# Self-attention of a two-layer block: the products of probabilities and values are put between the next transposes of probabilities, with both parts of the probabilities in one wide product

## What is computed

```python
def _layer(x, wqkv, qs, ksc, wo, ...):
    h = shift_token(x)                  # second half of the features comes from the token before
    q, k, v = split(h @ wqkv, 3)        # 8 heads of 64
    q = l2norm(q) * qs
    k = l2norm(k) * ksc
    q, k = rotary_xpos(q, k)
    o = local_attention(q, k, v)        # a query sees the 256 keys before it and its own
    x = x + o @ wo
    ...                                 # layer norm, w1, gelu gate, w2
```

## Time and profile before

| | |
|---|---|
| time, median of 3 runs | 3539.25 us (3538.21 to 3539.43) |
| time of the profiled execution | 3536.69 us |
| its span | 3534.9 us |
| PE busy | 3405.1 us, 96% |
| PEld busy | 2790.6 us, 79% |
| DVE busy | 1950.2 us, 55% |
| ACT busy | 1701.9 us, 48% |
| POOL busy | 1135.6 us, 32% |
| mean granted TensorE clock | 0.991 of full speed |

### The profile page before, as it was taken

How to read it: one execution, slowest core, us unless ns; L and a number is a source line. 1 busy time by engine, 2 the same in 40 slices (tenths; PEclk the granted TensorE clock), 3 DMA queues, 4 the chain that set the end, 5 groups by cost and what they waited for, 6 DMA issues and landing times. The chain is left out here.

```text
span 3534.9 us, 56378 instructions
## 1 busy us (share of the span) xinstructions
PE 3405.1 (96%) x20560; PEld 2790.6 (79%) x20560; DVE 1950.2 (55%) x4487; ACT 1701.9 (48%) x4490; POOL 1135.6 (32%) x1011
## 2 busy tenths in 40 slices
PE   6999998999999999999999979999999899999999
PEld 5666676788888877888888868888888778888887
DVE  6888876777777764222332257776777543323232
ACT  5666664777677762111111147776777521111111
POOL 3433434555555520000000045555555121110011
PEclk9999999999999999999999999999999999999999
DMA  4112204111111132011111111111111421101111
GB/s 124 42 46 65 72 34 135 49 61 61 61 61 61 61 97 93 29 41 44 44 43 44 65 66 61 61 61 61 61 61 58 129 93 50 49 34 50 50 34 37
DMA packets 186917, 216.26 MB, mean 61 GB/s; under 512 B 27142, under 2 KB 125702, under 8 KB 186643
## 3 DMA queue, kind: packets, MB, share of 16 engines
q1 hardware_dynamic: 186643, 212.65, 18.8%
HBM read 125.79 MB, written 69.00 MB: 55 GB/s over the span
## 5 line engine op out<-in xcount | busy, mean ns | idle before, releaser
L1981 DVE SCALAR_TENSOR_TENSOR u_full<-banks,b_cols,gate 128x512 f32<-128x512 f32 (+1 forms) x176 | 132.1, 751 | 876.7 <-ACT gate L1939 802.5
L1939 ACT ACTIVATE gate<-banks,b_cols 128x512 f32<-128x512 f32 (+1 forms) x176 | 121.3, 689 | 1010.8 <-PE banks L48 1010.8
L46 PE MATMUL banks<-fxT_h,w_h 128*128 128x512 f32 (+1 forms) x1408 | 556.7, 395 | 3.1 <-DVE w_l L1965 2.4
L48 PE MATMUL banks<-fxT_h,w_l 128*128 128x512 f32 (+1 forms) x1408 | 556.8, 395 | 0.0
L47 PE MATMUL banks<-fxT_l,w_h 128*128 128x512 f32 (+1 forms) x1408 | 556.0, 395 | 0.0
L1834 POOL TENSOR_TENSOR sums<-sums,b_rows 128x512 f32<-128x512 f32 x64 | 85.5, 1368 | 877.8 <-DMA sums<-z_rows 877.8
L46 PE MATMUL banks<-wqkv_h,hT_h 128*128 128x512 f32 x768 | 323.8, 422 | 9.7 <-DVE hT_l L1497 7.6
L46 PEld LDWEIGHTS banks<-fxT_h,w_h 128*128 128x128 f32 (+1 forms) x1408 | 260.2, 185 | 70.8 <-DVE w_l L1965 3.7
L48 PEld LDWEIGHTS banks<-fxT_h,w_l 128*128 128x128 f32 (+1 forms) x1408 | 260.8, 185 | 67.4
L47 PEld LDWEIGHTS banks<-fxT_l,w_h 128*128 128x128 f32 (+1 forms) x1408 | 260.4, 185 | 67.1
L48 PE MATMUL banks<-wqkv_h,hT_l 128*128 128x512 f32 x768 | 303.7, 395 | 0.0
(11 more groups left out here) (192 smaller groups left out, 8084.0 us busy)
## 6 DMA issues: line engine op xcount, KB each, us to landing
y_rows<-sums SPq DMA_DIRECT2D x16, 1024.0 KB
sums<-y_rows SPq DMA_DIRECT2D x64, 256.0 KB, 2.9
z_rows<-sums SPq DMA_DIRECT2D x64, 256.0 KB, 2.0
sums<-z_rows SPq DMA_DIRECT2D x16, 1024.0 KB, 5.6
thirds<-in_w SPq DMA_DIRECT2D x30, 512.0 KB, 5.0
thirds<-in_x SPq DMA_DIRECT2D x8, 1024.0 KB, 6.9
thirds<-y_rows SPq DMA_DIRECT2D x64, 128.0 KB, 2.7
thirds<-y_late SPq DMA_DIRECT2D x64, 128.0 KB, 3.3
```

What stands on the lines that cost most here:

```text
L46: pe.matmul(out, a_h, b_h, start=start, stop=False)
L48: return pe.matmul(out, a_l, b_h, start=False, stop=stop)
L1939: e.activation(gate[r, :], ps[r, 2 * (m % 2) + 1, :], ACT.Gelu, bias=b1[r, place[m], 1:2]).then_inc(s["ac_g"], 1)
L1981: e.scalar_tensor_tensor(out=u_full[r, m % 2, :], in0=ps[r, 2 * (m % 2), :], scalar=b1[r, place[m], 0:1], in1=gate[r, :], op0=ALU.add, op1 ...
```

## The change

Only the order and the shape of work in self-attention change, and one semaphore in the feed-forward part.

- `pT` becomes one tensor that holds high part and rest side by side (`[P, 4, 2, KEYS]`). For each key block, `weigh` makes one matmul of the high part of v by 256 columns, which are both parts of the probabilities; `weigh_rest` makes one of v's rest by 128 columns (the high part). The two results lie side by side in PSUM and take two banks instead of one, so `lo_o` now takes four VectorE instructions a half instead of two: it subtracts the high part into `o_rest`, and then adds the second result.
- `turn_and_weigh(t, half)` takes the place of four `transpose_p` and four `values`. Between the transposes of tile t, half 1 it puts the values of half 0 of the same tile; between those of half 0 the values of half 1 of the tile before.
- TensorE's list in tile t becomes: turn_and_weigh(t, 0), transpose_qk(t+1) for k, project(t+2, 0), scores(t+1, 0), project(t+2, 1), turn_and_weigh(t, 1), output(t-1), scores(t+1, 1), transpose_qk(t+2) for q, project(t+2, 2), transpose_h(t+3). At the end a `turn_and_weigh(NT, 0)` with values alone stands between two halves of output(30).
- PSUM banks are dealt out anew, `v` has five slots, and the lists of ScalarE and VectorE are rearranged to fit.
- In the feed-forward part the matmuls of the first factor no longer raise a semaphore of their own (`pe_a`).

```diff
-        pT = [sb(f"pT_{x}", [P, 4, KEYS], F32R) for x in "hl"]
+        pT = sb("pT", [P, 4, 2, KEYS], F32R)
+        o_rest = sb("o_rest", [P, 2, P])
...
-                def transpose_p(t, h):
-                    n = HEADS * t + h
-                    e.wait_ge(s["ac_p"], nth(LH, n + 1))
-                    e.wait_ge(s["dv_s"], nth(LH, min(n + LANES + 1, LH)))
-                    for k in range(first_block(t), 3):
-                        last = e.transpose(ps[:, bank_head(h), k * P:(k + 1) * P], prob[:, n % 4, k * P:(k + 1) * P], ident[:])
-                    last.then_inc(s["pe_t"], 1)
-                def values(t, h):
...
-                    for k in range(first_block(t), 3):
-                        slot = (t + 2 + k) % 4
-                        last = split_matmul(e, ps[0:DH, O_BANK, (h % 4) * P:(h % 4 + 1) * P],
-                                            [x[:, slot, h * DH:(h + 1) * DH] for x in v],
-                                            [x[:, n % 4, k * P:(k + 1) * P] for x in pT], k == first_block(t), k == 2)
+                def weigh(t, h, k):
+                    n = HEADS * t + h
+                    out = ps[0:DH, O_BANK + h % LANES // 2, h % 2 * 2 * P:(h % 2 + 1) * 2 * P].rearrange("p (x t) -> p x t", x=2)
+                    e.matmul(out, v[0][:, (t - 2 + k) % V_SLOTS, h * DH:(h + 1) * DH], pT[:, n % 4, :, k * P:(k + 1) * P],
+                             start=k == first_block(t), stop=False)
+                def weigh_rest(t, h, k):
+                    n = HEADS * t + h
+                    last = e.matmul(ps[0:DH, O_BANK + h % LANES // 2, h % 2 * 2 * P:h % 2 * 2 * P + P],
+                                    v[1][:, (t - 2 + k) % V_SLOTS, h * DH:(h + 1) * DH], pT[:, n % 4, 0, k * P:(k + 1) * P],
+                                    start=False, stop=k == 2)
...
+                def turn_and_weigh(t, half):
+                    tv, half_v = (t, 0) if half else (t - 1, 1)
+                    behind = None
+                    for h in range(LANES * half, LANES * half + LANES):
+                        n = HEADS * t + h
+                        hv = h % LANES + LANES * half_v
+                        if t < NT:
+                            e.wait_ge(s["ac_p"], nth(LH, n + 1))
+                            e.wait_ge(s["dv_s"], nth(LH, min(n + LANES + 1, LH)))
+                        for k in range(3):
+                            if t < NT and k >= first_block(t):
+                                last = e.transpose(ps[:, bank_head(h), k * P:(k + 1) * P], prob[:, n % 4, k * P:(k + 1) * P], ident[:])
...
+                            if tv >= 0 and k >= first_block(tv):
+                                if behind is not None:
+                                    weigh_rest(*behind)
+                                if k == first_block(tv):
+                                    e.wait_ge(s["dv_t"], nth(LH, HEADS * tv + hv + 1))
...
+                                weigh(tv, hv, k)
+                                behind = (tv, hv, k)
+                    if behind is not None:
+                        weigh_rest(*behind)
...
+                    turn_and_weigh(t, 1)
+                    output(t - 1, 0, DC // 2)
                     if t == NT - 1:
-                        output(t - 1)
...
+                        turn_and_weigh(NT, 0)
+                    output(t - 1, DC // 2, DC)
+                    scores(t + 1, 1)
+                    transpose_qk(t + 2, 0)
+                    project(t + 2, 2)
+                    transpose_h(t + 3)
+                output(NT - 1, 0, DC)
...
                     for odd in range(2):
-                        src = ps[0:DH, O_BANK, :].rearrange("p (c o t) -> p c o t", c=2, o=2)[:, :, odd, :]
                         r = slice(DH * odd, DH * odd + DH)
-                        ins = e.tensor_tensor(oT[1][r, t % 2, 2 * half:2 * half + 2, :], src,
-                                              oT[0][r, t % 2, 2 * half:2 * half + 2, :].bitcast(F32), ALU.subtract)
+                        e.tensor_tensor(o_rest[r], results(odd, 0), oT[0][r, t % 2, 2 * half:2 * half + 2, :].bitcast(F32),
+                                        ALU.subtract).then_inc(s["dv_or"], 1)
+                    for odd in range(2):
+                        e.wait_ge(s["dv_or"], nth(4 * NT, 4 * t + 2 * half + odd + 1))
+                        r = slice(DH * odd, DH * odd + DH)
+                        ins = e.tensor_tensor(oT[1][r, t % 2, 2 * half:2 * half + 2, :], results(odd, 1), o_rest[r], ALU.add)
...
                     for h in range(LANES, HEADS):
                         lo_p(t, h)
+                    normalise(t + 2, 1)
+                    lo_o(t, 0)
+                    residual(t - 1)
                     recip(t + 1, 0)
+                    masked(t + 1, 4)
+                    masked(t + 1, 5)
                     recip(t + 1, 1)
-                    normalise(t + 2, 1)
+                    masked(t + 1, 6)
+                    masked(t + 1, 7)
+                    lo_qk(t + 2, 0)
```

More of the change, by code:

```diff
@@ L1580, in _ @@
                 norms(1, 1)
-                lo_qk(0)
+                lo_qk(0, 0)
+                lo_qk(0, 1)
                 normalise(1, 0)
@@ L1600, in _ @@
                     if t:
-                        lo_qk(t + 1)
+                        lo_qk(t + 1, 1)
+                    lo_o(t - 1, 1)
                     if t == NT - 1:
@@ L1604, in _ @@
                     recip(t, 2)
-                    recip(t, 3)
                     norms(t + 2, 0)
                     if t == 0:
-                        lo_qk(t + 1)
-                    for h in range(LANES):
-                        masked(t + 1, h)
-                    lo_o(t, 0)
+                        recip(t, 3)
+                        lo_qk(1, 0)
+                        lo_qk(1, 1)
+                    masked(t + 1, 0)
+                    masked(t + 1, 1)
+                    if t:
+                        recip(t, 3)
+                    masked(t + 1, 2)
+                    masked(t + 1, 3)
                     normalise(t + 2, 0)
```

226 lines of the change are left out of this document (117 added, 109 removed).

## The result

The changed kernel takes 3547.16 us, the median of 14 runs (3545.01 to 3551.8). The kernel before, run on the same chip in between, takes 3538.03 us (3534.99 to 3539.43, 14 runs). The ratio is 1.0028, with a 95% interval from 1.002 to 1.0037: slower by 9 us, a little more than the 0.2% that I called measurable. The forecast was 3542 in a range of 3522 to 3560. As a change it was small, +3 us; measured are +9.1.

The account below looks back on a forecast made before the run. TensorE's own work was taken to bound full tiles, with waits at the phase's ends. Terms -2.6 - 2 + 1 + 5 = +1.4 us a phase, +3 for both, on 3539.5, plus 2.6 for the median: 3542 us, range 3522 to 3560.

Parts of the forecast that it names:

- the sum: Whole kernel: all terms added, +1.4 us a phase and +3 for both, giving 3542 us; chance 0.46.
- Full tiles, -2.6: 26 full tiles of a self-attention phase: 0.1 us less of 22.2 each, -2.6 us a phase, bounds 0 and -5.
- I cost a transpose at 109 ns in either order: TensorE's transposes: each occupies the array for 109 ns, so interleaving with values hides nothing.
- The wide product, 118 ns and worth 0.05 us a tile: Values in full tiles: one 256-column product takes 118 ns, replacing two of 60; 24 blocks save 0.05 us a tile.
- changing between kinds costs more: Rival, blocks of transpose, wide and narrow product: 10 ns more a block, +7 us a phase, 3557 us; chance 0.07.
- No new waits in full tiles: Full tiles: VectorE's additional 1.74 us a tile stays beside TensorE's work, with 0.3 us to spare; cost nothing.
- the rival of a late VectorE: Rival, full tiles: VectorE's chain late, each tile waits; at 0.6 us longer +8 us a phase, 3558 us; chance 0.20.
- the other two: Rivals: milder start and end, 3524 us, chance 0.21; transposes paced by weight loads that vanish, 3472 us, chance 0.06.
- Start, -2 and tiles 16 and 17, +1: Phase start: two waits go, -2 us (bounds -4.5, +1); second sequence: q's rotation late, +1 us (bounds 0, +2).
- End, +5 with bounds +2 and +8: End of the phase, tile 31: waits for VectorE and a half-level clock move products' end from 1304.1 to 1309.3 us.
- Both phases alike, +1.4 each: Both self-attention layers: the second repeats the first, so the +1.4 us a phase counts twice, +3 for both.
- The feed-forward, nothing: Feed-forward part: it only loses a semaphore that no engine waited for in addition, worth nothing.

Follow-up runs that it names:

- e11: e8 with only 64 of each 128 probability columns taken as transpose weights, half of the keys left out (for times alone): 3548.0 us, one run.
- e7: The changed kernel with each wide product of 256 columns made as two of 128 columns: 3578.43 us, ratio 1.0112.
- e10: e7 with only 64 of each 128 probability columns taken as transpose weights, half of the keys left out (for times alone): 3555.11 us, one run.
- e9: The changed kernel with a half tile's transposes grouped ahead of its products, and each wide product made as two of 128 columns: 3551.88 us, ratio 1.0038.
- e8: The changed kernel with all twelve transposes of a half tile first and its products behind them: 3546.11 us, ratio 1.0019.
- e5: The changed kernel with 28 unused matmuls of 512 columns added between tile 31's two half tiles: 3545.42 us, ratio 1.002.
- e4: The kernel before without the semaphore pe_a in the feed-forward part, nothing else changed: 3535.61 us, ratio 0.9995.
- e2: The changed kernel with the feed-forward's moments and normalisation moved later in VectorE's list at the end of the phase: 3546.13 us, ratio 1.0024.
- e6: e2 with 17 unused matmuls of 512 columns added in TensorE's stop in tile 31: 3536.24 us, ratio 0.9998.
- e1: The changed kernel with output(30) whole again ahead of the transposes of tile 31's second half, not split around the last values: 3552.18 us, ratio 1.0042.

## Why the prediction was right, and where its terms were off

The forecast was the sum, 3542, with an own range of 3532 to 3552; the kernel took 3547. That it lies inside is partly the width of the range: the change itself came out three times as large as the sum's +3 us. And the base, the median of three runs (3539.25), was 1.2 us above that of all 14 (3538.03), which brought the forecast nearer by luck. Its steps, for the first self-attention, against the trace:

- **Full tiles, -2.6.** Measured 22.13 against 22.22 us a tile, -2.4 for 26. The size was right, the reasons only in part. A transpose behind a transpose takes 109 ns whatever its weights, as I read from 104 columns, and e11 shows it with 64. But "nothing beside it can be hidden" and "I cost a transpose at 109 ns in either order" leave out the reverse: alternating can uncover a weight load that was covered. The Trainium skill ("TensorE: Matmul & The Clock Gate", section on LDWEIGHTS) says that a load's time goes by its columns. I had set that rule aside; as to time per transpose in a row the measurement decides against it. Behind a product of 60 ns e7 and e10 agree with it in kind: the weight columns count there, for 26 ns a block (0.62 us / 24). By the Trainium skill's rule it would be 47, an estimate from its 107 ns for 128 columns less the 60.
- **The wide product, 118 ns and worth 0.05 us a tile.** Its own duration was right (0.12 us). Its worth was not: 0.13 us in a row, and 0.62 where it stands ahead of a transpose. In this change the wide product pays for the alternation: with e9 as the base (22.18) alternating adds 0.57 and widening takes 0.62. The rival "changing between kinds costs more" has the right place with the wrong partner.
- **No new waits in full tiles.** Right; the rival of a late VectorE fell, though VectorE's share grew by 2.1 us a tile and not 1.74. So did the other two: the ends were not milder, and transposes kept their 109 ns (e8, e11).
- **Start, -2 and tiles 16 and 17, +1.** Measured -1.1 and +0.5 (the start of the table, 96.08 against 98.87, less the 1.7 us of work that only moved; in the second layer the start gives -0.5). The waits of 2.71 and 1.81 us went, and scores for pT (2.27) and the transposes behind them for the rotation (1.97) took over, more than I had counted; the granted clock of this stretch also fell from 0.93 to 0.86, which the sum had left out.
- **End, +5 with bounds +2 and +8.** This is the mis-sized term: +7.0 in the first layer (68.59 against 59.93, less the same 1.7). The stop ahead of the second half's transposes was 6.80 us ("some 7"), the one ahead of output(31) 2.44 ("some 2.6"), the half clock 1.34 (1.6; by e5). What I missed is a third wait of 1.74 us between: I wrote "half of output 1.38, values alone 2.1" without asking whose result banks these values overwrite. The next half tile's first product needs lo_o(31, 0) to have read them.
- **A row misread.** I took the 1.97 us of twelve transposes as a sign of the half clock. The granted clock there is 1.00; after every three the next head is waited for (starts 0.23 us apart in place of 0.11). The half level of the kernel before comes behind them, from 1286 to 1292 us (0.55 above).
- **Both phases alike, +1.4 each.** The four terms measured make -1.1 - 2.4 + 0.5 + 7.0 = +4.0 in the first, where the phase is 3.9 us longer. The second is 6.0 us longer: 1.5 of the 2.1 us more, since the kernel before kept the full clock at its end there, and 0.6 by the starts.
- **The feed-forward, nothing.** -0.9 us in all, of which e4's distances give the semaphore 0.8.

## What to carry to other kernels

Look at how long the matmul ahead of a wide weight load is: products that cost nothing extra in a row cost 26 ns each time when two short ones stood ahead of a transpose with 128 weight columns, and one wide product removed that. Interleaving two kinds of work gained nothing here, where transposes in a row were no faster with fewer weight columns; look for such rows first. At the end of a phase follow each result bank to its next writer, and don't count a shorter stop as gained before the granted clock behind it has been read: in e2 the 2.5 us were all taken back, and in e6 matmuls without use kept the gain, in seven runs of eleven.

## What the runs showed of the hardware

- The clock falls and rises differently behind equal waits: 1.65 us in tile 30 brought 0.61 in e8 and 1.00 in the changed kernel (1.63); behind 2.44 us ahead of output(31) the clock fell to the half level in e2 and e5 and stayed at the full one in e6 and in the changed kernel, in both layers each.
- At the half level a transpose's start follows the last by 0.213 us (e8's twelve in 2.82 us), a block of the changed kernel takes 0.53, and a matmul of 512 columns 0.43 (e1's output(31)).
- The additional semaphore cost the feed-forward 0.05 us in each group of 92.46 (e4), though VectorE, which waited for it, waits right behind for a later one.
